# Selective scan: GpSimd forms a row's inputs for two channel blocks in one instruction, with its products four steps late and other buffer counts

## Chip, cores and metric

The kernel runs on one core of a Trainium2 chip. The metric is the device time of one execution in microseconds; of the kernel before there are three, of which the median stands in the table below.

## What is computed

The reference chains four layers over a stream of 1,024 rows of 256: grouped attention, a mixture of experts, a pair of Mamba passes (one forward, one over the reversed sequence), and a feed-forward layer whose weights are looked up in a table of 16 values. The change lies in the Mamba passes. Cut to that:

```python
def _selective_scan(xi, dt, Bm, Cm, A, D):        # per sequence: DI = 512 channels, DS = 16 states
    def step(h, inp):
        dt_t, B_t, C_t, x_t = inp
        dA = jnp.exp(dt_t[..., None] * A)
        h = dA * h + (dt_t * x_t)[..., None] * B_t[:, None, :]
        y = jnp.einsum('bds,bs->bd', h, C_t)
        return (h, y)
    ...
    return ys + xi * D
# around it: dt = softplus(dtr @ dt_w.T + dt_b);  y = scan(...) * silu(z);  y @ out_w.T
```

## The kernel before

**The scan's steps.** The 512 channels are four blocks of 128 partitions; the time axis of the four sequences is laid out in halves of 512 columns (two sequences of 256). Direction (2) times half (2) gives four segments, `seg`. A segment has 64 steps (`SSTEP`), and a step is one state of one channel block: an instruction of 128x512. Steps come in pairs of blocks: `place(n)` (L1026) says that 32 steps (`PSTEP`, called a pair) alternate between two blocks, b = 0 and b = 1, and go through the 16 states; two neighbouring steps share one row r = n // 2, since B and C are the same for both blocks. There are 256 steps and 128 rows. The steps of a segment's first 32 work on blocks 0 and 1, the others on blocks 2 and 3.

**One step through the engines.** ScalarE writes the decay exp(dt·A) into one of three PSUM banks, `da` (L1727 and L1728). GpSimd forms the input `uB` = u · B (L1649), where u = dt · x and the row of B was copied to all partitions by a DMA into `RB`. VectorE runs the recurrence along the row with one scan instruction, in place in `da` (L1799) or into `hS` in SBUF (L1796). The state is multiplied by the row of C (`RC`): on VectorE from `da` into `hV` (L1741) or, for the steps that `on_pool` (L1011) picks, on GpSimd from `hS` into `hP` (L1658). TensorE adds the product to the output bank `ya` with an identity matmul (L1818).

**What orders the work.** Each engine has one queue, written out by hand, and counts on semaphores. GpSimd issues the input of step n, then the product of step n - `LATE` where that is its own; it forms an input once the scan of step n - `UBUF` has ended. VectorE issues scan n, then `product(n-1)` if that is its own. ScalarE may write `da` n when step n - 3 has left the bank: after its scan, if GpSimd has the product, or else after VectorE's product. `hP` has `PBUF` buffers, `hV` has `CBUF`, `hS` has two. SyncE issues the row loads in one queue: B of row i, then C of row i - 2 (L1613 to L1623); a row buffer is refilled when both its steps are through.

```python
ROWS = 4
UBUF, CBUF, PBUF, DABUF = 3, 3, 2, 3
LATE = 2
def on_pool(n):
    return n % 8 in (1, 4, 6) and n % PSTEP < PSTEP - LATE      # 11 of 32 steps
```

**Work beside it.** Between the steps the engines carry out the next segment's preparation (`side_tensor`, `side_scalar`, `side_vector`), hung on step numbers: projections and convolution on TensorE, copies and activations on ScalarE (with table loads where SiLU takes turns with exp and log, L1324 and L1328), and on VectorE `softplus` (L1559: `dt` from its parts, then `u`, L1562 and L1564), `out_vector` and one `table_vector` (L1552, a subtraction of two SBUF tiles) at step 56 of the last segment. `gate` (L1743) multiplies a finished `ya` with silu(z) at steps 2 and 3 of the next 32. `xi`, `sz`, `dt` and `u` are held twice, by the parity of the segment.

Of the kernel before, what the change touches and what calls it, by code (L numbers as in the profile page):

```python
# [14 lines left out]
ALU = mybir.AluOpType  # L15
# [963 lines left out]
ROWS = 4  # L979
UBUF, CBUF, PBUF, DABUF = 3, 3, 2, 3  # L980
LATE = 2
# [29 lines left out]
def on_pool(n):  # L1011

    return n % 8 in (1, 4, 6) and n % PSTEP < PSTEP - LATE

# [7 lines left out]
def vector_steps(n):  # L1022
    return n - pool_steps(n)


def place(n):  # L1026

    pair = n // PSTEP
    return n // SSTEP, pair, 2 * (pair % 2) + n % 2, n % 2, n // 2, n // 2 % ROWS

# [36 lines left out]
def mamba(c, g, dram, wt, ws, acc, hh, hl, sc):  # L1067
# [16 lines left out]
    s_rb, s_rc = ([sem(f"row_{n}{i}") for i in range(ROWS)] for n in "bc")  # L1084
# [4 lines left out]
    with ExitStack() as ctx:  # L1089
# [270 lines left out]
        def keep_dt(e, k, d):  # L1360
            e.wait_ge(s_u, DB * k + d + 1)
            e.activation(dt[:, k % 2, d, :], DTB[d][:, :], ACT.Copy).then_inc(s_dtc, 1)
# [196 lines left out]
        def softplus(e, k, d):  # L1559
            e.wait_ge(s_ln, DB * k + d + 1)  # L1560
            e.wait_ge(s_mx, DB * k + d + 1)
            e.tensor_tensor(DTB[d][:, :], DTB[d][:, :], u[:, k % 2, d, :], ALU.add).then_inc(s_dt, 1)  # L1562
            e.wait_ge(s_dt, DB * k + d + 1)
            e.tensor_tensor(u[:, k % 2, d, :], DTB[d][:, :], xi[:, k % 2, d, :], ALU.mult).then_inc(s_u, 1)  # L1564
# [39 lines left out]
        with nc.Block() as block:  # L1604
            @block.sync
            def _(e):

                mamba_weights(c, dram, "bm", ws[1])
                rows = STEPS // 2
                row = lambda r, at: dram["bc"][at + r % DS:at + r % DS + 1, half_of(r // (SSTEP // 2))].broadcast_to([P, HALF])  # L1610
                for i in range(rows + BEHIND):
                    if i < rows:
                        if i % (SSTEP // 2) == 0:  # L1613
                            e.wait_ge(s_bc, 16 * (i // (SSTEP // 2) + 1))
                        if i >= ROWS:
                            e.wait_ge(s_ub, 2 * (i - ROWS) + 2)
                        e.dma_start(RB[:, i % ROWS, :], row(i, 0)).then_inc(s_rb[i % ROWS], 16)
                    r = i - BEHIND
                    if r >= 0:
                        if r >= ROWS:  # L1620
                            e.wait_ge(s_hv, vector_steps(2 * (r - ROWS) + 2))
                            e.wait_ge(s_hp, pool_steps(2 * (r - ROWS) + 2))
                        e.dma_start(RC[:, r % ROWS, :], row(r, DS)).then_inc(s_rc[r % ROWS], 16)  # L1623

            @block.gpsimd
            def _(e):
                e.memset(raw[:, :, :, 0:PADC], 0.0).then_inc(s_pad, 1)
                e.memset(raw[:, :, :, PADC + SEQ:], 0.0).then_inc(s_pad, 1)
                e.memset(sc.zero[:, :], 0.0).then_inc(s_pad, 1)

                e.wait_ge(s_cs, (DCONV - 1) * DB)
                e.wait_ge(s_dg, DB * PADC)
                for w in ws:
                    e.wait_ge(w.ready, w.count)
                    for d in range(DB):
                        e.tensor_scalar(w.dD[:, d, :], g.ident[:, :], w.Dv[:, d:d + 1], None,
                                        ALU.mult).then_inc(s_dd, 1)
                e.tensor_tensor(g.x[:, :, :], g.x[:, :, :], wt.b_out[:, :].unsqueeze(1).broadcast_to([P, NB, D]),
                                ALU.add).then_inc(s_res, 1)
                for n in range(STEPS + LATE):  # L1640
                    if n < STEPS:
                        seg, pair, d, b, r, q = place(n)
                        if n % PSTEP < 2:
                            e.wait_ge(s_u, DB * seg + d + 1)
                        if b == 0:
                            e.wait_ge(s_rb[q], 16 * (r // ROWS + 1))
                        if n >= UBUF:
                            e.wait_ge(s_sc, n - UBUF + 1)
                        e.tensor_tensor(uB[:, n % UBUF, :], u[:, seg % 2, d, :], RB[:, q, :],  # L1649
                                        ALU.mult).then_inc(s_ub, 1)  # L1650
                    m = n - LATE
                    if m >= 0 and on_pool(m):
                        k, (r, q) = pool_steps(m), place(m)[4:]
                        e.wait_ge(s_rc[q], 16 * (r // ROWS + 1))
                        e.wait_ge(s_sc, m + 1)
                        if k >= PBUF:
                            e.wait_ge(s_ap, k - PBUF + 1)
                        e.tensor_tensor(hP[:, k % PBUF, :], hS[:, k % 2, :], RC[:, q, :],  # L1658
                                        ALU.mult).then_inc(s_hp, 1)

            @block.scalar
            def _(e):
# [48 lines left out]
                for n in range(STEPS):  # L1711
                    seg, pair, d, b, r, q = place(n)
# [15 lines left out]
                    e.activation(to[:, :, rest], by_seq(dt[:, seg % 2, d, :])[:, :, rest], ACT.Exp,  # L1728
# [5 lines left out]
            def _(e):  # L1734
                def product(n):
                    k, (r, q) = vector_steps(n), place(n)[4:]
                    e.wait_ge(s_rc[q], 16 * (r // ROWS + 1))
# [3 lines left out]
                    e.tensor_tensor(hV[:, k % CBUF, :], da[n % DABUF][:, :], RC[:, q, :], ALU.mult).then_inc(s_hv, 1)  # L1741
# [38 lines left out]
                for n in range(STEPS):  # L1780
                    seg, pair, d, b, r, q = place(n)
# [7 lines left out]
                    e.wait_ge(s_ub, n + 1)  # L1789
                    way = slice(None) if seg < 2 else slice(None, None, -1)  # L1790
                    a = da[n % DABUF]
                    if on_pool(n):
                        k = pool_steps(n)
                        if k >= 2:
                            e.wait_ge(s_hp, k - 1)
                        e.tensor_tensor_scan(hS[:, k % 2, way], a[:, way], uB[:, n % UBUF, way], 0.0,  # L1796
                                             ALU.mult, ALU.add).then_inc(s_sc, 1)
                    else:
                        e.tensor_tensor_scan(a[:, way], a[:, way], uB[:, n % UBUF, way], 0.0,  # L1799
# [353 lines left out]
def build(nc, dram, out):  # L2153
    with ExitStack() as ctx:
# [62 lines left out]
        with ExitStack() as mm:  # L2217
# [19 lines left out]
            sc.xi, sc.sz, sc.dt, sc.u = (c.sb(mm, n, [P, 2, DB, HALF]) for n in ("xi", "sz", "dt", "u"))  # L2237
            sc.RB, sc.RC = c.sb(mm, "rows_B", [P, ROWS, HALF]), c.sb(mm, "rows_C", [P, ROWS, HALF])
            sc.uB, sc.hV, sc.hP = (c.sb(mm, n, [P, w, HALF]) for n, w in (("uB", UBUF), ("hV", CBUF), ("hP", PBUF)))
            sc.dtr = c.sb(mm, "dtr", [P, HALF])  # L2240
            sc.zero = c.sb(mm, "zero", [P, NHS])
            sc.hS, sc.e1 = c.over("hS", [P, 2, HALF], g.feat), c.over("e1", [P, 2, HALF], g.feat, skip=8 * HALF)
# [78 lines left out]
```

## Time and profile before

| what | value |
|---|---|
| runs of the kernel before | 1097.88, 1098.32, 1099.91 us; median 1098.32 us |
| profiled execution, its own time | 1099.44 us |
| its span in the profile | 1097.7 us |
| busy share of the span | PE 87%, DVE 80%, POOL 64%, ACT 51% |
| scan stage, first scan to last | 556.85 us to about 1017 us |
| mean granted TensorE clock | 0.953 |

The span is the time from the first to the last instruction in the profile; 1.7 us lie around it. PE is TensorE, DVE is VectorE, ACT is ScalarE, POOL is GpSimd, SPq is SyncE's DMA queue. The four layers run one after another, so the shares of the whole span average over stages; the scan stage, some 460 us, is read by itself. In the profile, a wait for several semaphores is put down to the one that the profile has coming last, and where that engine had long been done it was another.

### The profile page before, as it was taken

To read this page: it belongs to the slowest core of one execution; us is meant where nothing else is said; L and a number is where in the kernel's file an instruction comes from. 1 tells how busy PE (TensorE), PEld (TensorE's weight loads), DVE (VectorE), ACT (ScalarE), POOL (GpSimd) and SP (SyncE) were. 2 spreads that over 40 slices of the span, in tenths; PEclk is the share of its full clock that TensorE was granted. 3 is DMA by queue.
4 is the path that set the end of the run, shared out by engine and by line. 5 is a ranking of instruction groups with operands and counts; after the bars stand their busy time and mean duration, and the time that the engine had idled before them with its cause. 6 is when DMAs were issued, how large, how long until landed. Compare 5 with 4: busy or idle time off the path is not lost. (4 is left out here: it accounts for less than half of the span.)

```text
span 1097.7 us, 13218 instructions
## 1 busy us (share of the span) xinstructions
PE 959.0 (87%) x3836; PEld 600.4 (55%) x3836; DVE 873.2 (80%) x1136; ACT 560.8 (51%) x1204; POOL 703.3 (64%) x505
## 2 busy tenths in 40 slices
PE   5898867999999999995969977989889987787798
PEld 2566646888888888883424422433444342332487
DVE  3788677777778778776579899988998999999853
ACT  2687632333333333322667766766577467564141
POOL 3377623555555555541289799989998899999000
PEclk9899988999999999997979999989999899999999
DMA  3000025442442442313065555654545455664001
GB/s 102 1 2 0 1 110 152 123 134 82 119 134 88 112 134 94 108 39 91 13 161 155 163 152 145 147 161 142 153 140 157 125 146 154 153 154 115 0 1 39
DMA packets 60033, 115.32 MB, mean 105 GB/s; under 512 B 10400, under 2 KB 15776, under 8 KB 59856
## 3 DMA queue, kind: packets, MB, share of 16 engines
q1 hardware_dynamic: 58848, 112.87, 36.7%
q10 hardware_dynamic: 1136, 1.90, 0.5%
q8 instruction: 18, 0.29, 0.1%
q14 instruction: 31, 0.25, 0.1%
HBM read 113.24 MB, written 1.51 MB: 105 GB/s over the span
## 5 line engine op out<-in xcount | busy, mean ns | idle before, releaser
L1649 POOL TENSOR_TENSOR uB<-u,rows_B 128x512 f32<-128x512 f32 x256 | 320.4, 1282 | 17.1 <-DVE da L1799 13.7
L870 POOL TENSOR_TENSOR lutw<-lutw,lt 128x865 f32<-128x865 f32 x80 | 184.9, 2312 | 164.9 <-DVE lt L836 159.1
L1818 PE MATMUL ya<-hV,ident 128*128 128x512 f32 x336 | 189.6, 651 | 62.6 <-DVE hV L1741 61.9
L1799 DVE TENSOR_TENSOR_SCAN da<-da,uB 128x512 f32<-128x512 f32 x168 | 201.0, 1220 | 17.2 <-ACT da L1728 12.3
L1818 PEld LDWEIGHTS ya<-hV,ident 128*128 128x128 f32 x336 | 61.3, 201 | 158.9 <-DVE hV L1741 123.4
L1658 POOL TENSOR_TENSOR hP<-hS,rows_C 128x512 f32<-128x512 f32 x88 | 112.7, 1281 | 21.8 <-issue 8.5
L1727 ACT ACTIVATE da<-zero 128x2 f32<-128x2 f32 x256 | 43.0, 168 | 152.0 <-DVE hV L1741 151.7
L1796 DVE TENSOR_TENSOR_SCAN hS<-da,uB 128x512 f32<-128x512 f32 x88 | 106.7, 1212 | 16.0 <-ACT da L1727 7.5
L1741 DVE TENSOR_TENSOR hV<-da,rows_C 128x512 f32<-128x512 f32 x168 | 112.6, 671 | 0.0
L744 ACT ACTIVATE ah<-ups 128x1024 fp32r<-128x1024 f32 x40 | 41.2, 1029 | 130.0 <-DVE ups L832 130.0
L829 DVE TENSOR_TENSOR si<-gps,cwb 128x1024 f32<-128x1024 f32 x40 | 49.0, 1225 | 57.1 <-ACT gps L741 53.4
L1818 PE MATMUL ya<-hP,ident 128*128 128x512 f32 x176 | 93.6, 614 | 0.0
L1728 ACT ACTIVATE da<-dt,fm_A 128x510 f32<-128x510 f32 x128 | 86.2, 674 | 0.0
L1728 ACT ACTIVATE da<-dt,bm_A 128x510 f32<-128x510 f32 x128 | 86.1, 673 | 0.0
L741 ACT ACTIVATE gps<-gps 128x1024 f32<-128x1024 f32 x40 | 40.3, 1008 | 89.4 <-PE gps L880 89.4
L349 POOL TENSOR_TENSOR prob<-prob,ri 128x1024 f32<-128x1024 f32 x32 | 60.7, 1896 | 28.4 <-DVE ri L513 28.4
L880 PE MATMUL gps<-xh,wh 128*128 128x512 f32 x160 | 63.4, 396 | 5.6 <-DVE si L829 5.6
L584 ACT ACTIVATE prob<-sps,mx 128x256 f32<-128x256 f32 x128 | 59.0, 481 | 11.1 <-DVE mx L509 11.0
L832 DVE TENSOR_TENSOR ups<-ups,si 128x1024 f32<-128x1024 f32 x40 | 49.3, 1233 | 19.2 <-PE ups L880 19.2
L880 PE MATMUL gps<-xh,wl 128*128 128x512 f32 x160 | 63.0, 394 | 0.0
L880 PE MATMUL gps<-xl,wh 128*128 128x512 f32 x160 | 63.0, 394 | 0.0
L880 PE MATMUL ups<-xh,wh 128*128 128x512 f32 x160 | 62.3, 390 | 0.0
(341 smaller groups left out, 2034.8 us busy)
## 6 DMA issues: line engine op xcount, KB each, us to landing
rows_B<-bc_rows SPq DMA_DIRECT2D x128, 256.0 KB, 3.6
rows_C<-bc_rows SPq DMA_DIRECT2D x128, 256.0 KB, 4.3
wr<-in_moe_w SPq DMA_DIRECT2D x40, 384.0 KB, 4.8
cwb<-cw_rows SPq DMA_DIRECT2D x16, 512.0 KB, 4.0
cwb<-cw_rows SPq DMA_DIRECT2D x16, 384.0 KB, 5.0
cwb<-cw_rows SPq DMA_DIRECT2D x16, 256.0 KB, 4.1
lut_f<-in_lut_idx SPq DMA_DIRECT2D x1, 2160.0 KB, 10.3
cwb<-cw_rows SPq DMA_DIRECT2D x16, 128.0 KB, 4.4
```

Of the source, the lines that this page charges most:

```text
L349: e.tensor_tensor(prob[:, u % NP, :, :], prob[:, u % NP, :, :], ri[:, u, :].unsqueeze(2).broadcast_to([P, GROUPS, SEQ]), ALU.mult).then_in ...
L584: a = e.activation(prob[:, u % NP, gg, :], sps[:, u % 2, gg, :], ACT.Exp, bias=mx[:, u, gg:gg + 1], accum_out=rs[:, u, gg:gg + 1])
L832: e.tensor_tensor(ups[:, :], ups[:, :], si[:, s, :], ALU.mult).then_inc(s_a, 1)
L870: e.tensor_tensor(part, part, lt[:, q, :], ALU.add).then_inc(s_la, 1)
L880: mm = e.matmul(ps[:, half(h)], w[:, slot, o:o + P], x[:, q, half(h)], start=i == 0, stop=i == len(terms) - 1)
L1649: e.tensor_tensor(uB[:, n % UBUF, :], u[:, seg % 2, d, :], RB[:, q, :], ALU.mult).then_inc(s_ub, 1)
L1658: e.tensor_tensor(hP[:, k % PBUF, :], hS[:, k % 2, :], RC[:, q, :], ALU.mult).then_inc(s_hp, 1)
L1728: e.activation(to[:, :, rest], by_seq(dt[:, seg % 2, d, :])[:, :, rest], ACT.Exp, scale=ws[seg // 2].A[:, d, r % DS:r % DS + 1]).then_inc( ...
L1741: e.tensor_tensor(hV[:, k % CBUF, :], da[n % DABUF][:, :], RC[:, q, :], ALU.mult).then_inc(s_hv, 1)
L1796: e.tensor_tensor_scan(hS[:, k % 2, way], a[:, way], uB[:, n % UBUF, way], 0.0, ALU.mult, ALU.add).then_inc(s_sc, 1)
L1799: e.tensor_tensor_scan(a[:, way], a[:, way], uB[:, n % UBUF, way], 0.0, ALU.mult, ALU.add).then_inc(s_sc, 1)
L1818: return e.matmul(ya[n % 2][:, :], g.ident[:, :], at, start=False, stop=False, skip_group_check=True).then_inc(done, 1)
```

## The change

GpSimd's loop runs over rows, not steps: one instruction of 128 x (2 x 512) multiplies u of both blocks with the row of B, broadcast over the blocks. The products that GpSimd has are issued four steps behind, not two. `on_pool` picks other steps, 12 of 32 in place of 11. `dt` and `u` are held once. Buffers: B rows 4 to 3, C rows 4 to 5, inputs 3 steps to 3 rows (6 steps), `hV` 3 to 4, `hP` 2 to 3, `hS` 2 to 4; `da` stays at 3. `hS` gets its own memory, and `dtr` moves over `g.feat`.

```diff
-ROWS = 4
-UBUF, CBUF, PBUF, DABUF = 3, 3, 2, 3
-LATE = 2
+BROWS, CROWS = 3, 5
+UPAIRS, CBUF, PBUF, DABUF, HBUF = 3, 4, 3, 3, 4
+LATE = 4
...
-    return n % 8 in (1, 4, 6) and n % PSTEP < PSTEP - LATE
+    return n % PSTEP % 7 in (1, 3, 5) and n % PSTEP < PSTEP - LATE
...
-            e.activation(u[:, k % 2, d, :], DTB[d][:, :], ACT.Relu, ...)
+            e.activation(u[:, d, :], DTB[d][:, :], ACT.Relu, ...)
...
-                        if i >= ROWS:
-                            e.wait_ge(s_ub, 2 * (i - ROWS) + 2)
-                        e.dma_start(RB[:, i % ROWS, :], row(i, 0)).then_inc(s_rb[i % ROWS], 16)
+                        if i >= BROWS:
+                            e.wait_ge(s_ub, i - BROWS + 1)
+                        e.dma_start(RB[:, i % BROWS, :], row(i, 0)).then_inc(s_rb[i % BROWS], 16)
                     r = i - BEHIND
                     if r >= 0:
-                        if r >= ROWS:
-                            e.wait_ge(s_hv, vector_steps(2 * (r - ROWS) + 2))
-                            e.wait_ge(s_hp, pool_steps(2 * (r - ROWS) + 2))
+                        if r >= CROWS:
+                            e.wait_ge(s_hv, vector_steps(2 * (r - CROWS) + 2))
+                            e.wait_ge(s_hp, pool_steps(2 * (r - CROWS) + 2))
...
-                for n in range(STEPS + LATE):
-                    if n < STEPS:
-                        seg, pair, d, b, r, q = place(n)
-                        if n % PSTEP < 2:
-                            e.wait_ge(s_u, DB * seg + d + 1)
-                        if b == 0:
-                            e.wait_ge(s_rb[q], 16 * (r // ROWS + 1))
-                        if n >= UBUF:
-                            e.wait_ge(s_sc, n - UBUF + 1)
-                        e.tensor_tensor(uB[:, n % UBUF, :], u[:, seg % 2, d, :], RB[:, q, :],
-                                        ALU.mult).then_inc(s_ub, 1)
-                    m = n - LATE
-                    if m >= 0 and on_pool(m):
...
+                for r in range((STEPS + LATE) // 2):
+                    if 2 * r < STEPS:
+                        seg, pair, d = place(2 * r)[:3]
+                        if r % DS == 0:
+                            e.wait_ge(s_u, DB * seg + d + 2)
+                        e.wait_ge(s_rb[r % BROWS], 16 * (r // BROWS + 1))
+                        if r >= UPAIRS:
+                            e.wait_ge(s_sc, 2 * (r - UPAIRS) + 2)
+                        e.tensor_tensor(uB[:, r % UPAIRS, :, :], u[:, d:d + 2, :],
+                                        RB[:, r % BROWS, :].unsqueeze(1).broadcast_to([P, 2, HALF]),
+                                        ALU.mult).then_inc(s_ub, 1)
+                    for m in (2 * r - LATE, 2 * r - LATE + 1):
+                        if m >= 0 and on_pool(m):
+                            k, row = pool_steps(m), place(m)[4]
+                            e.wait_ge(s_rc[row % CROWS], 16 * (row // CROWS + 1))
+                            e.wait_ge(s_sc, m + 1)
+                            if k >= PBUF:
+                                e.wait_ge(s_ap, k - PBUF + 1)
+                            e.tensor_tensor(hP[:, k % PBUF, :], hS[:, k % HBUF, :], RC[:, row % CROWS, :],
+                                            ALU.mult).then_inc(s_hp, 1)
...
                     e.wait_ge(s_da, 2 * n + 2)
-                    e.wait_ge(s_ub, n + 1)
+                    e.wait_ge(s_ub, r + 1)
...
-                        if k >= 2:
-                            e.wait_ge(s_hp, k - 1)
-                        e.tensor_tensor_scan(hS[:, k % 2, way], a[:, way], uB[:, n % UBUF, way], 0.0,
+                        if k >= HBUF:
+                            e.wait_ge(s_hp, k - HBUF + 1)
+                        e.tensor_tensor_scan(hS[:, k % HBUF, way], a[:, way], uB[:, r % UPAIRS, b, way], 0.0,
...
-            sc.xi, sc.sz, sc.dt, sc.u = (c.sb(mm, n, [P, 2, DB, HALF]) for n in ("xi", "sz", "dt", "u"))
+            sc.xi, sc.sz = (c.sb(mm, n, [P, 2, DB, HALF]) for n in ("xi", "sz"))
+            sc.dt, sc.u = (c.sb(mm, n, [P, DB, HALF]) for n in ("dt", "u"))
```

## Rows read from the trace of the kernel before

**Rows 1.** Busy time of each engine in stretches; the second sums 18 stretches, 556.8 to 1018.
```profile
800.00:848.60 48.60, 46.88 (x117) 21.18 (x115) 43.60 (x48) 37.21 (x82) 45.69 (x37) 1.00 0.51 149
...
sum 461.20, PE 393.06 PEld 164.31 DVE 427.86 ACT 298.78 POOL 423.11; mean PE 21.84 PEld 9.13 DVE 23.77 ACT 16.60 POOL 23.51
```
**Rows 2.** Costliest groups of instructions, the scan's on POOL and DVE.
```profile
L1649 POOL TENSOR_TENSOR uB<-u,rows_B 128x512 f32<-128x512 f32 x256 | 320.4, 1282 | 17.1 <-DVE da L1799 13.7
...
L1799 DVE TENSOR_TENSOR_SCAN da<-da,uB 128x512 f32<-128x512 f32 x168 | 201.0, 1220 | 17.2 <-ACT da L1728 12.3
...
L1658 POOL TENSOR_TENSOR hP<-hS,rows_C 128x512 f32<-128x512 f32 x88 | 112.7, 1281 | 21.8 <-issue 8.5
...
L1741 DVE TENSOR_TENSOR hV<-da,rows_C 128x512 f32<-128x512 f32 x168 | 112.6, 671 | 0.0
```
**Rows 3.** Waits of DVE from 554 to 1018 us: total, times, longest.
```profile
DVE da L1799 <- ACT da L1728: 12.3, 8, 2.8
DVE hS L1796 <- ACT da L1727: 7.5, 19, 0.6
DVE hS L1796 <- issue: 6.5, 3, 2.5
DVE da L1799 <- POOL uB L1649: 2.8, 6, 1.3
DVE hS L1796 <- ACT da L1728: 1.8, 3, 0.8
DVE da L1799 <- ACT da L1727: 1.8, 6, 0.3
```
**Rows 4.** Timeline of DVE, 742 to 756: start, duration, instructions, [idle before].
```profile
743.62 0.67 DVE L1741 TENSOR_TENSOR hV<-da,rows_C 128x512 f32<-128x512 f32 x1
744.20 2.34 DVE L1799 TENSOR_TENSOR_SCAN da<-da,uB 128x512 f32<-128x512 f32 x2
746.44 0.68 DVE L1741 TENSOR_TENSOR hV<-da,rows_C 128x512 f32<-128x512 f32 x1
749.65 1.22 DVE L1796 TENSOR_TENSOR_SCAN hS<-da,uB 128x512 f32<-128x512 f32 x1 [2.53 <-issue]
...
754.56 1.22 DVE L1796 TENSOR_TENSOR_SCAN hS<-da,uB 128x512 f32<-128x512 f32 x1 [0.27 <-ACT da L1727]
```
**Rows 5.** Timeline of POOL, the same stretch.
```profile
747.07 1.27 POOL L1658 TENSOR_TENSOR hP<-hS,rows_C 128x512 f32<-128x512 f32 x1 [2.34 <-PE ya L1818]
748.30 3.72 POOL L1649 TENSOR_TENSOR uB<-u,rows_B 128x512 f32<-128x512 f32 x3
751.98 1.27 POOL L1658 TENSOR_TENSOR hP<-hS,rows_C 128x512 f32<-128x512 f32 x1
753.21 3.72 POOL L1649 TENSOR_TENSOR uB<-u,rows_B 128x512 f32<-128x512 f32 x3
```
**Rows 6.** Groups of POOL instructions by shape: other products and sums.
```profile
L870 POOL TENSOR_TENSOR lutw<-lutw,lt 128x865 f32<-128x865 f32 x80 | 184.9, 2312 | 164.9 <-DVE lt L836 159.1
...
L349 POOL TENSOR_TENSOR prob<-prob,ri 128x1024 f32<-128x1024 f32 x32 | 60.7, 1896 | 28.4 <-DVE ri L513 28.4
...
L1638 POOL TENSOR_TENSOR x<-x,b_out 128x2048 f32<-128x2048 f32 x1 | 4.5, 4521 | 0.0
```
**Rows 7.** Timeline of the scan's start.
```profile
554.26 5.16 POOL L1649 TENSOR_TENSOR uB<-u,rows_B 128x512 f32<-128x512 f32 x4 [3.17 <-DVE u L1564]
554.82 0.69 DVE L1564 TENSOR_TENSOR u<-side,xi 128x512 f32<-128x512 f32 x1
...
556.85 1.23 DVE L1799 TENSOR_TENSOR_SCAN da<-da,uB 128x512 f32<-128x512 f32 x1 [1.33 <-POOL uB L1649]
```
**Rows 8.** Timeline around step 56 of the last segment, DVE.
```profile
1003.25 3.64 DVE L1552 TENSOR_TENSOR lut_l<-lutw,lut_h 128x540 fp32r<-128x540 f32 x1
```
**Rows 9.** The same stretch, POOL.
```profile
1002.57 3.73 POOL L1649 TENSOR_TENSOR uB<-u,rows_B 128x512 f32<-128x512 f32 x3
```
**Rows 10.** DMA issues of the page: KB each, us from issue to landing.
```profile
rows_B<-bc_rows SPq DMA_DIRECT2D x128, 256.0 KB, 3.6
```

More of the change, by code:

```diff
@@ L1028, in place @@
     pair = n // PSTEP
-    return n // SSTEP, pair, 2 * (pair % 2) + n % 2, n % 2, n // 2, n // 2 % ROWS
+    return n // SSTEP, pair, 2 * (pair % 2) + n % 2, n % 2, n // 2
 def summed(pair):
@@ L1082, in mamba @@
         sem, "xb bcc bc xl lr dm ab e1 ln mx dt dtc u".split())
-    s_rb, s_rc = ([sem(f"row_{n}{i}") for i in range(ROWS)] for n in "bc")
+    s_rb, s_rc = ([sem(f"row_{n}{i}") for i in range(w)] for n, w in (("b", BROWS), ("c", CROWS)))
     s_da, s_ub, s_sc, s_hv, s_hp, s_av, s_ap, s_sk, s_g, s_om, s_oa = map(
@@ L1348, in parts @@
             e.activation(e1[:, d % 2, :], DTB[d][:, :], ACT.Abs, bias=ws[k // 2].dtb[:, d:d + 1]).then_inc(s_ab, 1)
-            e.activation(u[:, k % 2, d, :], DTB[d][:, :], ACT.Relu, bias=ws[k // 2].dtb[:, d:d + 1]).then_inc(s_mx, 1)
+            e.activation(u[:, d, :], DTB[d][:, :], ACT.Relu, bias=ws[k // 2].dtb[:, d:d + 1]).then_inc(s_mx, 1)
         def exp(e, k, d):
@@ L1361, in keep_dt @@
             e.wait_ge(s_u, DB * k + d + 1)
-            e.activation(dt[:, k % 2, d, :], DTB[d][:, :], ACT.Copy).then_inc(s_dtc, 1)
+            e.activation(dt[:, d, :], DTB[d][:, :], ACT.Copy).then_inc(s_dtc, 1)
         def silu_input(e, k):
@@ L1561, in softplus @@
             e.wait_ge(s_mx, DB * k + d + 1)
-            e.tensor_tensor(DTB[d][:, :], DTB[d][:, :], u[:, k % 2, d, :], ALU.add).then_inc(s_dt, 1)
+            e.tensor_tensor(DTB[d][:, :], DTB[d][:, :], u[:, d, :], ALU.add).then_inc(s_dt, 1)
             e.wait_ge(s_dt, DB * k + d + 1)
-            e.tensor_tensor(u[:, k % 2, d, :], DTB[d][:, :], xi[:, k % 2, d, :], ALU.mult).then_inc(s_u, 1)
+            e.tensor_tensor(u[:, d, :], DTB[d][:, :], xi[:, k % 2, d, :], ALU.mult).then_inc(s_u, 1)
         def side_vector(e, seg):
@@ L1711, in _ @@
                 for n in range(STEPS):
-                    seg, pair, d, b, r, q = place(n)
+                    seg, pair, d, b, r = place(n)
                     if n % SSTEP == 0:
@@ L1727, in _ @@
                     e.activation(to[:, :, first], sc.zero[:, :], ACT.Copy).then_inc(s_da, 1)
-                    e.activation(to[:, :, rest], by_seq(dt[:, seg % 2, d, :])[:, :, rest], ACT.Exp,
+                    e.activation(to[:, :, rest], by_seq(dt[:, d, :])[:, :, rest], ACT.Exp,
                                  scale=ws[seg // 2].A[:, d, r % DS:r % DS + 1]).then_inc(s_da, 1)
@@ L1735, in product @@
                 def product(n):
-                    k, (r, q) = vector_steps(n), place(n)[4:]
-                    e.wait_ge(s_rc[q], 16 * (r // ROWS + 1))
+                    k, r = vector_steps(n), place(n)[4]
+                    e.wait_ge(s_rc[r % CROWS], 16 * (r // CROWS + 1))
                     if k >= CBUF:
@@ L1740, in product @@
                     e.wait_ge(s_sc, n + 1)
-                    e.tensor_tensor(hV[:, k % CBUF, :], da[n % DABUF][:, :], RC[:, q, :], ALU.mult).then_inc(s_hv, 1)
+                    e.tensor_tensor(hV[:, k % CBUF, :], da[n % DABUF][:, :], RC[:, r % CROWS, :],
+                                    ALU.mult).then_inc(s_hv, 1)
                 def gate(pair, b):
@@ L1780, in _ @@
                 for n in range(STEPS):
-                    seg, pair, d, b, r, q = place(n)
+                    seg, pair, d, b, r = place(n)
                     if n % SSTEP == 0:
@@ L2236, in build @@
             sc.win_in, sc.xp_in = c.kept("win_in"), c.kept("xp_in")
-            sc.xi, sc.sz, sc.dt, sc.u = (c.sb(mm, n, [P, 2, DB, HALF]) for n in ("xi", "sz", "dt", "u"))
-            sc.RB, sc.RC = c.sb(mm, "rows_B", [P, ROWS, HALF]), c.sb(mm, "rows_C", [P, ROWS, HALF])
-            sc.uB, sc.hV, sc.hP = (c.sb(mm, n, [P, w, HALF]) for n, w in (("uB", UBUF), ("hV", CBUF), ("hP", PBUF)))
-            sc.dtr = c.sb(mm, "dtr", [P, HALF])
+            sc.xi, sc.sz = (c.sb(mm, n, [P, 2, DB, HALF]) for n in ("xi", "sz"))
+            sc.dt, sc.u = (c.sb(mm, n, [P, DB, HALF]) for n in ("dt", "u"))
+            sc.RB, sc.RC = c.sb(mm, "rows_B", [P, BROWS, HALF]), c.sb(mm, "rows_C", [P, CROWS, HALF])
+            sc.uB = c.sb(mm, "uB", [P, UPAIRS, 2, HALF])
+            sc.hV, sc.hP, sc.hS = (c.sb(mm, n, [P, w, HALF]) for n, w in (("hV", CBUF), ("hP", PBUF), ("hS", HBUF)))
             sc.zero = c.sb(mm, "zero", [P, NHS])
-            sc.hS, sc.e1 = c.over("hS", [P, 2, HALF], g.feat), c.over("e1", [P, 2, HALF], g.feat, skip=8 * HALF)
+            sc.dtr, sc.e1 = c.over("dtr", [P, HALF], g.feat), c.over("e1", [P, 2, HALF], g.feat, skip=8 * HALF)
             sc.bcr = c.over("bcr", [2 * DS, HALF], g.feat, skip=12 * HALF)
```

11 lines of the change are left out of this document (2 added, 9 removed).

## The prediction

> **What bounds the kernel now.** The change touches the scan stage alone, so I read that stage. The busy time by stretches comes first: of the 461 us from 556.8 to 1018, DVE is busy for 428 and POOL for 423 [rows 1]. Two engines in series, each at 92%, and some 33 us of idle time on DVE: the question is who ends it. The groups of instructions give the work [rows 2]: POOL does 256 inputs and 88 products at 1.28 us, DVE 256 scans at about 1.22 and 168 products at 0.67. An instruction starts a little before its predecessor's end, so I take pitches from the timelines. Two scans take 2.24 us from 744.20 to 746.44 and a product 0.58 from 743.62 to 744.20 [rows 4], so a scan costs DVE 1.12 us and a product 0.585. Three inputs take 3.68 from 748.30 to 751.98, and a product 1.23 from 751.98 to 753.21 [rows 5], so everything on POOL costs 1.23.
>
> Per step DVE then wants 1.12 + 168/256 x 0.585 = 1.50 us before its work beside the scan; POOL wants 344 x 1.23 / 256 = 1.65. POOL is the slower one wherever DVE has nothing else to do, and DVE wherever it has softplus, gates or a late decay. With inputs only three steps deep, neither can run ahead to cover the other.
>
> The waits of DVE say how much each costs, once their labels are corrected [rows 3]. The scan at 754.56 is put down to ACT's small copy (L1727), but the input that POOL began at 753.21 ends 1.28 later, at 754.49 [rows 4, 5]: that is what it waited for. The two scans that waited, 749.65 and 754.56, are 4.91 us apart, as are the beginnings of POOL's groups of inputs, 748.30 and 753.21: four POOL instructions, to the hundredth. So the 7.5 + 1.8 us under L1727 are waits for POOL. The 6.5 us in three waits named "issue" are too: before the one at 749.65, POOL's product had waited 2.34 us for TensorE to free one of two `hP` buffers, and the next input stood behind it in POOL's queue, from 748.30 to 749.5 [rows 4, 5]. Of the 2.8 us under uB, 1.33 are the start of the scan [rows 7] and 1.5 are POOL. In all **17.3 us of DVE's idle time are POOL's**. The 12.3 + 1.8 us under L1728 are real waits for ACT, mostly behind its SiLU and table loads (the longest is 2.8).
>
> **The change part by part.** *Inputs in pairs.* 256 instructions at 1.23 become 128 of 1,024 elements. No row has this instruction; its bounds are L349 with 1,024 elements but a second operand held constant along 256 columns, 1.90 us, and two of today's, 2 x 1.28 = 2.56 [rows 6, 2]. The nearest is L1638, which like the new one has a row broadcast over blocks: 2,048 elements in 4.52 us. The line through 512 at 1.282 and 2,048 at 4.521 has 2.109 ns per element and 0.20 us fixed, so 2.36 us, pitch 2.31. POOL falls by 128 x (2.46 - 2.31) = 19 us.
>
> *Twelve products of 32 in place of eleven.* 96 for 88: POOL gains 8 x 1.23 = 10 us of work, DVE loses 8 x 0.585 = **4.7 us**, all on the path where DVE sets the pace. POOL's total is 128 x 2.31 + 96 x 1.23 = 414 us (423 before); DVE's is 428 - 4.7 = 423. Per step POOL wants 1.62 and DVE 1.12 + 160/256 x 0.585 = 1.49.
>
> *Inputs three rows deep, products four steps late.* POOL may form the input of row r+1 when row r-2 is scanned, while DVE still has rows r-1 and r ready: about 2 x 3.1 = 6.2 us of DVE's work. In that time POOL needs at most one product and one input, 3.5 us. So it has 2.7 us to spare, against a lag of 0.13 us a step: 20 steps, and in 20 steps DVE has a softplus pair or a gate nearly everywhere in the schedule of work beside. With three `hP` buffers in place of two, POOL's product at 747.07 would not have waited for the last add but one. I remove all 17.3 us.
>
> *The start.* A first input now needs u of both blocks. The second u ends at 554.82 + 0.69 = 555.51, and the pair takes 2.36: 557.9, where the first scan began at 556.85 [rows 7]. That costs **1.1 us**. Later, both u are written at DVE's steps 23 to 25 and 52, 53, and POOL may take them from steps 28 and 60 on, so this wait is covered by two steps at least; if softplus came three steps later it would show.
>
> *Waits for ACT.* Three decay banks remain, so 14.1 us stay. But DVE will meet ACT's other side jobs where it met POOL before. Where a step on POOL stands between two on DVE, ACT has one scan, 1.12 us, from the bank's release to the next scan, and 11 such places in 32 become 12. The range is from nothing to the 8 us that half a microsecond at one place in six would make; I take **3 us**, nearer to nothing, since waits under L1728 outside the big ones are few today [rows 3].
>
> *Single dt and u.* ACT overwrites u and dt of block d some 15 steps after their last reader; costs nothing, and if it did wait, ACT would stand still with the decays behind it. *Row buffers.* B of row i is issued when the input of row i-3 ends, and wanted two inputs and at least one product later, 2 x 2.31 + 1.23 = 5.9 us; it lands in 3.6 [rows 10] and is ready. SyncE issues as many DMAs in the same order; the C row's wait, for row r-5's products, has always been met by then. `hS` and `dtr` change places only.
>
> *The table subtraction.* At 1003.25 DVE's subtraction of two SBUF tiles took 3.64 us [rows 8], while POOL ran three inputs from 1002.57 to 1006.30 [rows 9]: it ended 0.6 us after them. It waited until POOL stopped, through more than one instruction. With POOL's pieces longer, what POOL can still do before it needs a scan is from one product (1.2) to two pairs and two products (7.1); the wait was 2.9, so between -1.7 and +4.2, and I take **+1**. The Trainium skill (SBUF — State Buffer, SBUF: two separate sides) says that the shared port pair goes to whichever "starts first" for the whole instruction, with the other blocked. By that rule alone the wait would have ended with the first input at about 1003.85 and would now be at most one pair, 2.36 us, which makes the sum a microsecond or two lower; the trace agrees that one blocks, not that it lasts only one instruction.
>
> **The sum.** -17.3 - 4.7 + 1.1 + 3 + 1 = -16.9 us. The profiled span of 1097.7 becomes 1080.8 and that execution's 1099.44 becomes 1082.5. It stands 1.1 us above the median of 1098.32, so against the median I predict **1081.4 us**, 1.5% less. A measurement of this kernel can tell about 0.2% from no change.
>
> **The rivals.** *B, POOL remains the pacemaker.* If the pair costs two singles, POOL's total is 128 x 2.51 + 96 x 1.23 = 439 us; with perhaps a third of its 38 idle us left (12, around the start and ACT's long jobs) the stage is 451 against 461: 1088.5. For it speaks that today's price per element is 2.5 ns; against it, L1638's 2.2 and L349's 1.85.
>
> *C, another engine takes over.* From 800 to 848.6 TensorE is busy for 46.9 of 48.6 us at full clock [rows 1]; there are three such stretches, and its side work feeds ACT and so the decays. If it or ACT catches every wait that POOL leaves, only the 8 products and the start count: -3.6, 1094.7. Against it: TensorE idles in the other half of each segment, where most of the 17.3 us lie, and ACT is busy for 299 of 461 [rows 1].
>
> *D, slower.* The price of the pair decides. The 865-element sum of L870 takes 2.31 us [rows 6], 2.67 ns per element; at that, a pair is 2.74, POOL's total 128 x 2.69 + 118 = 462, with 12 idle 474: +13, or 1111 us. The point is a pair at 2.63 us. Against it: L870 stands beside other DVE work and in L1638 more elements take less each. The Trainium skill (Perfetto Trace Analysis, Optimizing Scalar/DVE Operations) warns that moving work between DVE and GpSimd "might not help", since they share a read port. Here DVE's scans and products read one operand from PSUM, and a product on DVE takes 0.67 us on the average of 168 [rows 2]; no run here shows them slowed.
>
> **The numbers.** The forecast 0.68, B 0.12, C 0.12, D 0.08. The forecast's own range is from 1074 (nothing for ACT, the table at its low end, POOL cheaper) to 1090 (8 for ACT, the table at its high end). The 8-in-10 range takes in B and stops short of C's centre and D: 1072 to 1094. All of the forecast and B, and most of C, are faster by over 0.2% (2.2 us): 0.88. Within 0.2%: 0.05, from C with a little more lost. Slower: 0.07.
>
> **What would show it.** Right: L1649's group x128 near 2.36 us; waits of scans named L1727, uB and "issue" down from 17.3 to a few us; waits named L1728 between 14 and 20; products on DVE x160; no long wait of POOL for TensorE ahead of an input. Wrong: a pair at 2.5 us or more, with POOL busy for over 95% of the stage; scans waiting for rows of B; DVE's products waiting for TensorE's adds, or the decays for TensorE's convolution between steps 10 and 30.

## The result, and the profile after

The changed kernel takes 1103.35 us (median of six runs, 1101.18 to 1104.36) against 1098.2 before: a ratio of 1.0043, 95% interval 1.0030 to 1.0055. I had forecast 1081.4 and a range of 1072 to 1094. It is slower, outside the range and on the other side.

The costliest groups of the page after (the same columns as in [rows 2]):

```profile
L1649 POOL TENSOR_TENSOR uB<-u,rows_B 128x1024 f32<-128x1024 f32 x128 | 301.1, 2361 | 15.3 <-DVE da L1801 10.7
...
L1801 DVE TENSOR_TENSOR_SCAN da<-da,uB 128x512 f32<-128x512 f32 x160 | 192.5, 1219 | 26.7 <-ACT da L1729 23.8
...
L1659 POOL TENSOR_TENSOR hP<-hS,rows_C 128x512 f32<-128x512 f32 x96 | 122.2, 1273 | 33.1 <-DVE hS L1798 24.8
...
L1742 DVE TENSOR_TENSOR hV<-da,rows_C 128x512 f32<-128x512 f32 x160 | 106.9, 669 | 0.0
```

The waits of DVE in the scan stage, from 554 to 1024 us, to be held against [rows 3]:

```profile
DVE da L1801 <- ACT da L1729: 23.8, 16, 2.7
DVE hS L1798 <- ACT da L1729: 14.4, 16, 1.7
...
DVE da L1801 <- POOL uB L1649: 2.5, 1, 2.5
```

And the waits of ACT in the same stretch, of which there were 5.9 us for PE before:

```profile
ACT e L1348 <- PE side L1205: 7.1, 3, 2.4
ACT sz L1313 <- PE side L1109: 6.6, 4, 2.2
ACT xi L1298 <- PE side L1132: 6.3, 10, 1.2
ACT bcr L1334 <- PE side L1177: 5.3, 3, 1.8
ACT dtr L1342 <- PE side L1188: 4.6, 3, 1.5
ACT raw L1292 <- PE side L1109: 4.3, 7, 1.3
```

GpSimd did all that was expected of it. The paired input takes 2.361 us (2.36 forecast), and the only wait for it that is left is the first of the scan. In its place VectorE waits 38.2 us for ScalarE's exponentials, the decays (L1729; it was L1728, 14.1 us). ScalarE has no more work than before (busy for 297.8 us of the stage, 298.8 before); it stands 34.2 us before TensorE's side results, and the next decay stands behind it in its queue.

The timeline of PE at the beginning of the second segment after the change shows where that begins:

```profile
679.14 1.12 PE L1820 MATMUL ya<-hV,ident 128*128 128x512 f32 x2 [1.38 <-DVE hV L1742]
683.79 2.08 PE L1820 MATMUL ya<-hV,ident 128*128 128x512 f32 x2 [3.52 <-DVE hV L1742]
685.66 1.91 PE L1205 MATMUL side<-dtr,wdt 128*128 128x512 f32 x2
687.37 1.39 PE L1875 MATMUL ya<-xi,fm_dD 128*128 128x512 f32 x2
```

ScalarE and VectorE at that place, also after the change:

```profile
687.61 0.69 ACT L1348 ACTIVATE e<-side,fm_dtb 128x512 f32<-128x512 f32 x1 [2.35 <-PE side L1205]
```

```profile
689.58 1.23 DVE L1801 TENSOR_TENSOR_SCAN da<-da,uB 128x512 f32<-128x512 f32 x1 [1.30 <-ACT da L1729]
```

And PE at the same place before:

```profile
680.42 1.12 PE L1818 MATMUL ya<-hV,ident 128*128 128x512 f32 x2 [1.39 <-DVE hV L1741]
681.39 1.02 PE L1873 MATMUL ya<-xi,fm_dD 128*128 128x512 f32 x2
682.24 1.02 PE L1818 MATMUL ya<-hV,ident 128*128 128x512 f32 x2
683.10 1.02 PE L1205 MATMUL side<-dtr,wdt 128*128 128x512 f32 x2
```

TensorE's side work hangs on the number of adds done (`side.advance(pair % 2 * PSTEP + i)`), not on the step. `summed` puts a GpSimd product's add `LATE` steps behind. With `LATE` = 2 the third add is that of step 3; with `LATE` = 4 and the new places it is that of step 4, the fourth that of step 5 (was 3), the fifth that of step 6 (was 5). Counted out over 32 adds, they come 0.8 step later on the average, and the side work with them. Here the third dt matmul (L1205) comes only behind the add of step 4, after a gap of 3.5 us. ScalarE waits 2.35 us for it (the row at 687.61), VectorE 1.30 for the next decay (689.58). The same wait of ScalarE stands at the beginning of the third and the fourth segment.

### The profile page after: what moved, and what is told of

It is laid out like the page before. It is cut to its first block and busy times, and to the rows that moved or that the text cites. A ratio compares the mean times of both kernels' runs of the same rounds, so it can differ in the third digit from the quotient of the medians.

```text
span 1102.6 us, 13081 instructions
## 1 busy us (share of the span) xinstructions
PE 959.8 (87%) x3836; PEld 602.7 (55%) x3836; DVE 869.6 (79%) x1128; ACT 561.1 (51%) x1204; POOL 694.1 (63%) x385
## 5 line engine op out<-in xcount | busy, mean ns | idle before, releaser
L1649 POOL TENSOR_TENSOR uB<-u,rows_B 128x1024 f32<-128x1024 f32 x128 | 301.1, 2361 | 15.3 <-DVE da L1801 10.7
L1820 PE MATMUL ya<-hV,ident 128*128 128x512 f32 x320 | 181.4, 652 | 72.0 <-DVE hV L1742 72.0
L1801 DVE TENSOR_TENSOR_SCAN da<-da,uB 128x512 f32<-128x512 f32 x160 | 192.5, 1219 | 26.7 <-ACT da L1729 23.8
L1820 PEld LDWEIGHTS ya<-hV,ident 128*128 128x128 f32 x320 | 57.9, 199 | 162.3 <-DVE hV L1742 127.6
L1659 POOL TENSOR_TENSOR hP<-hS,rows_C 128x512 f32<-128x512 f32 x96 | 122.2, 1273 | 33.1 <-DVE hS L1798 24.8
L1798 DVE TENSOR_TENSOR_SCAN hS<-da,uB 128x512 f32<-128x512 f32 x96 | 116.1, 1209 | 14.6 <-ACT da L1729 14.4
L1728 ACT ACTIVATE da<-zero 128x2 f32<-128x2 f32 x256 | 42.8, 167 | 128.1 <-DVE hV L1742 126.0
L1742 DVE TENSOR_TENSOR hV<-da,rows_C 128x512 f32<-128x512 f32 x160 | 106.9, 669 | 0.0
L1820 PE MATMUL ya<-hP,ident 128*128 128x512 f32 x192 | 103.0, 619 | 0.0
L1729 ACT ACTIVATE da<-dt,fm_A 128x510 f32<-128x510 f32 x128 | 86.3, 674 | 0.0
L1729 ACT ACTIVATE da<-dt,bm_A 128x510 f32<-128x510 f32 x128 | 86.2, 673 | 0.0
L584 ACT ACTIVATE prob<-sps,mx 128x256 f32<-128x256 f32 x128 | 59.0, 481 | 11.1 <-DVE mx L509 11.0
L832 DVE TENSOR_TENSOR ups<-ups,si 128x1024 f32<-128x1024 f32 x40 | 49.3, 1233 | 19.3 <-PE ups L880 19.2
```

Source lines behind the costliest of these rows:

```text
L584: a = e.activation(prob[:, u % NP, gg, :], sps[:, u % 2, gg, :], ACT.Exp, bias=mx[:, u, gg:gg + 1], accum_out=rs[:, u, gg:gg + 1])
L832: e.tensor_tensor(ups[:, :], ups[:, :], si[:, s, :], ALU.mult).then_inc(s_a, 1)
L1649: e.tensor_tensor(uB[:, r % UPAIRS, :, :], u[:, d:d + 2, :], RB[:, r % BROWS, :].unsqueeze(1).broadcast_to([P, 2, HALF]), ALU.mult).then_i ...
L1659: e.tensor_tensor(hP[:, k % PBUF, :], hS[:, k % HBUF, :], RC[:, row % CROWS, :], ALU.mult).then_inc(s_hp, 1)
L1729: e.activation(to[:, :, rest], by_seq(dt[:, d, :])[:, :, rest], ACT.Exp, scale=ws[seg // 2].A[:, d, r % DS:r % DS + 1]).then_inc(s_da, 1)
L1798: e.tensor_tensor_scan(hS[:, k % HBUF, way], a[:, way], uB[:, r % UPAIRS, b, way], 0.0, ALU.mult, ALU.add).then_inc(s_sc, 1)
```

## The experiments

Theory T1: the lag of that count makes the change slow. Rivals: T2, TensorE is simply full; T3, the new places of GpSimd's steps free the decay banks late. Times are medians; the kernel before stood at 1097.8 to 1098.6 beside them, and ratios are to it. "The decay's waits" are VectorE's waits for ScalarE's exponentials.

**1. Side work one add earlier.**

```diff
-                        side.advance(pair % 2 * PSTEP + i)
+                        side.advance(pair % 2 * PSTEP + min(i + 1, PSTEP - 1))
```

> The changed kernel, with TensorE's side work hung one add earlier in each 32 steps. Theory T1 (TensorE's side jobs are counted in adds; with products four steps late the count lags the steps by up to two, so ScalarE stands before TensorE's results and the decays come late): ScalarE's waits for TensorE's side results fall from 34 us to under 15, VectorE's waits for the decay exponential from 38 us to 18 to 25, time 1083 to 1092. T2 (TensorE is simply full in the stretches with projection and convolution): nothing comes earlier, the same waits within 5 us, time 1099 to 1105. T3 (it is the places of GpSimd's steps, each alone between two of VectorE's, which free the decay banks late): waits stay, time 1100 to 1105.

1088.9 us, ratio 0.9920 [0.9904, 0.9937]: 14.5 less than the change. ScalarE's waits for TensorE are 8.2 us, VectorE's for the decay 20.6. As T1 has it, waits and time; T2 and T3, each as the whole cause, have no room for this.

**2. Products two steps late.**

```diff
-LATE = 4
+LATE = 2
-    return n % PSTEP % 7 in (1, 3, 5) and n % PSTEP < PSTEP - LATE
+    return n % PSTEP % 7 in (1, 3, 5) and n % PSTEP < PSTEP - 4
```

> The changed kernel with GpSimd's products two steps late, not four (the same 12 steps of 32, all other buffer counts kept). T1: TensorE's count of adds follows the steps again; VectorE's waits for the decay exponential fall to 18 to 25 us, time 1083 to 1092, perhaps with some 5 us more of waits for GpSimd, which runs one row less ahead. T2 and T3: VectorE's waits for the decay stay at 33 us or more, time 1098 to 1106.

1099.1 us, 1.0013 [0.9999, 1.0026]. The time lies in the range of T2 and T3, the waits are T1's. ScalarE's waits for TensorE fell to 6.2 us and the decay's (L1729) to 17.9, as T1 says, but GpSimd now stood 41.8 us before its products for scans just under way, and the inputs behind them came late. The waits of its DVE from 554 us on, where the small ones labelled L1728 are again GpSimd's:

```profile
DVE da L1801 <- POOL uB L1649: 11.7, 19, 2.5
DVE da L1801 <- ACT da L1729: 9.8, 5, 2.7
DVE hS L1798 <- ACT da L1729: 8.1, 8, 1.7
DVE hS L1798 <- ACT da L1728: 6.6, 12, 0.6
```

So with the new places the four steps are needed for GpSimd's lead, and harm TensorE's count.

**3. The pairs without the rest** (old places, products two steps late, old counts of `hV`, `hP`, `hS`).

```diff
-UPAIRS, CBUF, PBUF, DABUF, HBUF = 3, 4, 3, 3, 4
-LATE = 4
+UPAIRS, CBUF, PBUF, DABUF, HBUF = 3, 3, 2, 3, 2
+LATE = 2
-    return n % PSTEP % 7 in (1, 3, 5) and n % PSTEP < PSTEP - LATE
+    return n % 8 in (1, 4, 6) and n % PSTEP < PSTEP - LATE
```

> The paired inputs and their three rows of buffers, single dt and u and the row buffers of the change, but the old 11 steps of 32, products two steps late, and the old counts of hV, hP and hS. T1: waits for the decay near the 14 us of before, GpSimd's waits mostly gone but for the ones behind two hP buffers (6.5 us); 8 products more on VectorE than in the change: 1083 to 1090. T2: 1098 to 1104. T3: as T1, since the old places are back: 1083 to 1090, so this run tells T2 from the other two, and the run with products two steps late tells T1 from T3.

1092.75 us, 0.9946 [0.9930, 0.9963]; ScalarE waits 4.6 us for TensorE. The pairs alone gain 5.5 us, outside the 1083 to 1090 that I had written: the decay's waits are 17.4 us, not near 14, and 8.4 us of GpSimd's are left behind the first scan. It speaks against T2, which wanted 1098 to 1104.

**4. The new places alone**, in the kernel before.

```diff
-    return n % 8 in (1, 4, 6) and n % PSTEP < PSTEP - LATE
+    return n % PSTEP % 7 in (1, 3, 5) and n % PSTEP < PSTEP - 4
```

> The kernel before with the 12 steps of 32 of the change and nothing else. GpSimd sets the pace there and gets 8 products of 1.23 us more, so up to 10 us slower. T1 and T2: 1102 to 1109, with VectorE's waits for the decay exponential (the true ones) within 4 us of the 14 of before. T3: the true waits for the decay grow by 10 us or more, time 1109 or above.

1113.0 us, 1.0130 [1.0113, 1.0147], slower than any branch of the text but T3's, whose mark, 10 us more of waits for the decay, is missing: they are 17.6 us (14.1 before), and ScalarE waits 1.9 for TensorE. Waits that are GpSimd's rose by 12 us, as the pacemaker got 10 us more work. A part of T3 is real, and has its row, here in this run and in the kernel before: the wait behind the gate's SiLU, three times in each.

```profile
685.66 1.22 DVE L1796 TENSOR_TENSOR_SCAN hS<-da,uB 128x512 f32<-128x512 f32 x1 [1.70 <-ACT da L1728]
```

```profile
683.20 1.23 DVE L1799 TENSOR_TENSOR_SCAN da<-da,uB 128x512 f32<-128x512 f32 x1 [1.12 <-ACT da L1728]
```

Step 3 of the 32 is now GpSimd's, and VectorE has a product less to cover ScalarE. Here GpSimd sets the pace and hides what the places cost otherwise; runs 5 to 8 show more of it.

**5. Old places in the change** (27 added, so 11 of 32, none in the last four), **6. with side work one add earlier, 7. two adds earlier; 8. new places, two adds earlier.**

```diff
-    return n % PSTEP % 7 in (1, 3, 5) and n % PSTEP < PSTEP - LATE
+    return (n % 8 in (1, 4, 6) or n % PSTEP == 27) and n % PSTEP < PSTEP - LATE
-                        side.advance(pair % 2 * PSTEP + i)
+                        side.advance(pair % 2 * PSTEP + min(i + 1, PSTEP - 1))
```

The first part is the edit of run 5; two adds earlier has `i + 2` in the second.

> The changed kernel with GpSimd's steps at the old places (n % 8 in 1, 4, 6, to which step 27 is added, so 11 of 32, none in the last four); products four steps late as in the change. T1: the count of adds still lags, so ScalarE still waits over 20 us for TensorE and the time is 1096 to 1105, 8 products more on VectorE included (5 us). T3 (the new places are the cause): waits for the decay back to 14 to 18 us, 1084 to 1090.

> Old places as in the run before this, and TensorE's side work hung one add earlier. T1 with a smaller part for the places (the alternation of the new ones lengthens the wait behind the gate's SiLU from 1.13 to 1.70 us, and others of its kind): 1086 to 1092, the 5 us of 8 more products nearly made up by 3 to 4 us less of waits for the decay. T3 as a large part: under 1084.

> The changed kernel with the old places and TensorE's side work two adds earlier. One add earlier gave 1084.1 us with 2 us of ScalarE's waits for TensorE left, so no lag remains: the decays' waits stay at 11 us, and adds that come later behind side work lengthen the gates' waits (7.5 us now). 1083 to 1089, no better than 1084.1.

> The changed kernel, with TensorE's side work hung two adds earlier. Hung one add earlier it gave 1088.9 us and left 11 us of ScalarE's waits for TensorE. T1 (the count): those fall further, VectorE's waits for the decay exponential from 20.6 to 15 to 18 us, 1084 to 1088. T2 (TensorE full in the dense stretches): no further gain, and side work ahead of the adds makes gates and GpSimd's product buffers wait longer: 1088 to 1095.

In this order: 1091.9, 1084.1, 1086.75 and 1086.0 us; ratios 0.9948 [0.9932, 0.9964], **0.9870 [0.9848, 0.9893]**, 0.9889 [0.9873, 0.9905], 0.9874 [0.9843, 0.9904]. With the change and run 1 they make a table; each field has the time, the decay's waits and ScalarE's waits for TensorE, in us. The times are medians, the waits those of the profiled execution, which was the slowest for runs 7 and 8 (1089.4 and 1090.0 us).

| side work | new places | old places |
|---|---|---|
| as in the change | 1103.35; 38.2; 34.2 | 1091.9; 19.0; 18.7 |
| one add earlier | 1088.9; 20.6; 8.2 | 1084.1; 11.1; 1.7 |
| two adds earlier | 1086.0; 23.1; 3.4 | 1086.75; 6.2; 3.5 |

Run 5 lies between T1's 1096 and T3's 1090: the places act on the count too, which I had not worked out. With the old ones the third add is that of step 3 again, and the 2.35 us before L1205 are gone; 18.7 us of ScalarE's waits are left, and the shift takes them to 1.7. The average lag there is 0.7 step, counted as above, hardly less than the new places' 0.8: what matters is which adds are late, not the average.

Run 6 is faster than T1's branch (1086 to 1092) and stands at the edge of "T3 as a large part" (under 1084). Run 8 has T1's time, but not its waits: the decay's were to fall to 15 to 18 and are 23.1, although ScalarE hardly waits for TensorE any more. So with the lag mostly out of the way the new places still cost waits for the decay: 9.5 us one add earlier (20.6 against 11.1), twice what their eight products fewer on VectorE save, hence 1088.9 us against 1084.1; and 16.9 us two adds earlier, where ScalarE waits as little for TensorE with either (there VectorE stands longer before GpSimd and the gates with the old ones, and the times are equal). The wait behind the gate's SiLU, step 5 of the 32, is 1.70 us three times in runs 1 and 8, whatever the shift, and 0.6 us twice in run 6. With the old places two adds earlier buys nothing beyond one (run 7, as expected in its time). Run 6 is the fastest kernel of this study and beats both. Its DVE's waits:

```profile
DVE da L1801 <- ACT da L1729: 11.1, 10, 2.7
DVE sz L1751 <- issue: 6.5, 5, 2.8
DVE da L1801 <- POOL uB L1649: 2.5, 1, 2.5
```

**9. TensorE with less to do.** Two of the convolution's three matmuls are left out in segments 1 to 3.

```diff
                 if t:
                     yield
+                if t < PADC - 1:
+                    continue
```

> The changed kernel with two of the convolution's three diagonal matmuls left out on TensorE in segments 1 to 3 (that part of the computation is left out, all waits and yields stay), some 7 us less of TensorE's work in each dense stretch. T2 (TensorE full): ScalarE's waits for TensorE go in those stretches, time 1090 or less. T1: only the waits for the convolution's own results shrink (6.3 us), while those at the beginning of a segment, where TensorE has idle time, stay: 1096 to 1101.

1098.2 us, 1.0004 [0.9992, 1.0015]. Of ScalarE's 34.2 us before TensorE 26.8 stay. Those for the convolution (L1132, 6.3 us) are gone, and those for L1205 at a segment's beginning stay: 2.35, 2.35 and 2.21 us, against 2.35, 2.35 and 2.36. As T1 has it; T2 falls, which wanted 1090 or less.

**10. and 11. The kernel before, with side work one add later and one earlier.**

```diff
-                        side.advance(pair % 2 * PSTEP + i)
+                        side.advance(pair % 2 * PSTEP + (max(i - 1, 0) if i < PSTEP - 1 else i))
```

> The kernel before with nothing changed but that TensorE's side work hangs one add later. Counted, the change ran its adds 0.8 step later than the kernel before on the average of 32; this run puts that lag into the kernel before. T1: ScalarE's waits for TensorE rise from 6 us to 20 or more and the time by 6 to 14 us, to 1104 to 1112. If something else in the change was the cause: within 3 us of 1098.

> The kernel before with TensorE's side work hung one add earlier. There GpSimd sets the pace and ScalarE waits only 6 us for TensorE: 1096 to 1099, no gain beyond 2 us. If side work one add earlier were a gain of its own, whatever the change: under 1092, and the good times of the runs with the shift would not speak for the lag.

1094.95 us (0.9975 [0.9963, 0.9987]) and 1107.6 us (1.0083 [1.0063, 1.0103]): both against what I had written. The link is there: one add later, ScalarE waits 20.6 us for TensorE in place of 5.9 and the decay's waits go from 14.1 to 21.7. But the three waits named "issue", 6.5 us, that came of GpSimd standing before two `hP` buffers [rows 3, 5] fell to 0.4, as the adds come ahead of the side work. One add earlier it is the reverse: ScalarE never waits for TensorE, and "issue" is 11.3 us. GpSimd's own waits for TensorE's adds go the same way, 5.5 us before, 3.0 one add later and 14.4 one add earlier. Early side work pays only where GpSimd has buffers to spare.

**12. Inputs two rows deep** in the fastest version (`UPAIRS` = 2).

> Old places, TensorE's side work one add earlier (1084.1 us), and inputs two rows deep instead of three. If the depth of the inputs is what removed VectorE's waits for GpSimd: they come back to 10 us or more, 1092 to 1100. If the cheaper instruction did (2.36 us for two inputs in place of 2.56): 1084 to 1087.

1098.3 us, 1.0000 [0.9987, 1.0012], 14.2 more than with three. It is the depth that pays, not the cheaper instruction: GpSimd has the same 2.36 us an input, and waits 53 us for scans to free one (16.5 with three rows). Some 9 us of VectorE's waits for it are back, a little under the 10 of the first branch.

**13. Gates a step later** in the fastest version (`GATE_AT` = 3).

> Old places, side work one add earlier, and the gates one step later (steps 3 and 4 of the next 32), since VectorE still stood 7.5 us before gates for TensorE's last adds. If it only waits for the adds: half of that goes, 1080 to 1083. If the next 32 steps' adds, which wait for the gate to free the bank, then fill hV's four buffers: 1084 to 1090.

1086.4 us, 0.9886 [0.9863, 0.9908], in the second branch. The gates' waits fall from 7.5 to 4.6 us, the decay's rise from 11.1 to 15.1. Nothing gained.

**14. ScalarE's side jobs a step later**, TensorE as in the change.

```diff
-                    side.advance(n % SSTEP)
+                    side.advance(n % SSTEP - 1)
```

> The changed kernel with ScalarE's side jobs one step later and TensorE's program untouched. If ScalarE stands before TensorE's late results and holds up the decays (T1): its waits for TensorE's side results fall from 34 us to 10 to 20, VectorE's waits for the decay exponential from 38 to 22 to 30, time 1089 to 1097. If earlier side work on TensorE helped in another way (adds, gates, product buffers): ScalarE's jobs later only push its results out, 1101 to 1107.

1102.3 us, 1.0040 [1.0027, 1.0052]. The waits moved as T1 said, the time, in the other branch's range, did not: ScalarE's for TensorE 34.2 to 17.5, VectorE's for the decay 38.2 to 17.2. But VectorE's own side jobs, whose due steps were left, now stand before ScalarE's results:

```profile
DVE acc L1557 <- PE side L1218: 6.8, 5, 2.0
DVE wl_in L1546 <- ACT wh_in L1284: 5.1, 4, 2.1
...
DVE side L1562 <- ACT side L1358: 3.8, 9, 0.8
```

The side work is one timetable over three engines.

**15. The count restored**: after each add, as much side work as the old order of adds had released by that step.

```diff
+                was = times(lambda n: n % 8 in (1, 4, 6) and n < PSTEP - 2, 2)
+                due = [sum(t <= now for t in was) - 1 for now in times(on_pool, LATE)]
...
-                        side.advance(pair % 2 * PSTEP + i)
+                        side.advance(pair % 2 * PSTEP + due[i])
```

(`times(on, late)` lists the step at which each add is issued.)

> The changed kernel with TensorE's side work at the step numbers that it had in the kernel before: after each add, as much of it as the old order of adds had released by that step. T1, with the lag of the count as the whole of it: ScalarE's waits for TensorE under 12 us, VectorE's waits for the decay exponential 16 to 22 us, 1084 to 1091. If one add earlier gained by more than undoing the lag: 1092 or above, clearly worse than 1088.9.

1095.8 us, 0.9975 [0.9966, 0.9985]: 7.6 of the 14.5 us, and outside T1's branch. ScalarE's waits for TensorE are 19.5 us (under 12 expected), the decay's 27.2 (16 to 22). The count could not be restored everywhere: step 3 no longer has an add, so what was due there still waits for step 4's, and the 2.35 us before L1205 stand in it unchanged. By the other branch one add earlier gains by more than undoing the lag; no run separates the two.

**16. One job earlier**: L1205 due at add 1 in segments 1 to 3 (`yield 2` to `yield 1` in `side_tensor`), all else as in the change.

> The changed kernel with one side job of TensorE in each of segments 1 to 3, the matmul for dt of block 2, due at add 1 in place of add 2, so before the gap behind the gate's SiLU. If that gap with the lowered clock is what makes the results late at the beginning of a segment: ScalarE's wait of 2.35 us for it (7.1 in all) goes, with it VectorE's waits of 1.30 us at that place (three) and perhaps part of the next ones (1.45): 1096 to 1100. If the waits at that place come from elsewhere: 1101 to 1105.

1096.4 us, 0.9984 [0.9974, 0.9994]: 7 us less than the change, for one job moved in three segments. ScalarE's waits for L1205 are gone and its others stay (27.0 us in all); the decay's are 33.7 us, 4.5 less. The rows at the gap:

```profile
678.27 1.02 PE L1205 MATMUL side<-dtr,wdt 128*128 128x512 f32 x2
682.04 1.24 PE L1820 MATMUL ya<-hV,ident 128*128 128x512 f32 x2 [2.75 <-DVE hV L1742]
```

## Why the prediction was wrong

*The pair.* Right: 2.361 us against 2.36, from the line through 512 and 2,048 elements.

*The 17.3 us.* Right, and so was reading L1727 and "issue" as GpSimd's: none of them is left in the change. It takes the depth: with two rows some 9 us of such waits are back (run 12).

*Products.* x160 of 669 ns, so 4.7 us of work less, right; but the same places cost more in waits (below). *The start.* The second u ends at 556.31 and the scan begins at 558.83, 1.98 us later than before; 0.8 of that lies ahead of the stage, where nothing was changed, 1.2 is the pair (1.1 forecast).

*The table subtraction.* 5.82 us in place of 3.64: +2.2 (+1 taken, within the bounds).

*Waits for ACT.* **This is the step that failed: 3 us taken, 8 at most allowed, 24.1 measured.** I had worked out when a decay bank comes free and looked for ScalarE's own work ahead of it; the 3 us were for that. I costed "products four steps late" on GpSimd's queue alone, though the same constant sets the order of TensorE's adds, and the adds are the clock of its side work. What the diff moved on TensorE's queue, some 110 side matmuls a segment by 0.8 step, was in no term. My rival C had the right sign of trouble and a wrong reason, that TensorE be full (run 9), and its price, at most what GpSimd gave back, was a bound that doesn't exist: a late job holds up ScalarE, ScalarE the decay, and VectorE stands although GpSimd is ready. The prediction's own sign of it, decays that wait for the convolution between steps 10 and 30, came in a small part: 6.3 of ScalarE's 34.2 us are for L1132.

The terms as measured: -17.3 - 4.7 + 1.2 + 24.1 + 2.2 + 0.8 ahead of the stage = +6.3 us; the span rose by 4.9. The 1.4 between them I leave open.

Of the waits for the decay the lag of the count is the greater part: one add earlier takes 17.6 of the 38.2 us away, and 14.5 us of time. The other part is in the term as I had it, and mis-sized: a step on GpSimd gives ScalarE less cover, which is read from the rows behind the SiLU (runs 1, 4, 6 and 8) and was not tested by itself. With side work one add earlier the new places have 9.5 us more of these waits than the old ones (runs 1 and 6), where I had taken 3 and allowed 8, and the eight products moved to GpSimd win nothing back. The two parts start from 11.1 us, the waits of run 6, not from the 14.1 before; and the split is that of this order, since the places move the count as well (run 5: taken first, they are 19.2 us and the count 7.9). Runs 10 and 11 set the limit of the theory: the lag costs its full price only where GpSimd no longer paces the scan.

## What to carry to other kernels

When one engine's schedule is counted in its own instructions, a change of their order is a change of its clock: list at which step each add falls, old and new, and which job hangs on it, before pricing the change. A wait that goes on the pacing engine is gained only if every queue that feeds the next bound keeps its dates; look there first for who stands in order ahead of the critical instruction. And buffers, lateness and due steps are one setting: here the change with nothing else but the old places and side work one add earlier goes from 0.4% slower to 1.3% faster.

## What the runs showed of the hardware

VectorE's subtraction of two SBUF tiles (L1552) waited through three further GpSimd instructions, beyond the one under way when it began. DVE, then POOL, of the changed kernel around 1006 us:

```profile
1006.29 5.82 DVE L1552 TENSOR_TENSOR lut_l<-lutw,lut_h 128x540 fp32r<-128x540 f32 x1
```

```profile
1006.75 1.26 POOL L1659 TENSOR_TENSOR hP<-hS,rows_C 128x512 f32<-128x512 f32 x1
1007.98 2.33 POOL L1649 TENSOR_TENSOR uB<-u,rows_B 128x1024 f32<-128x1024 f32 x1
1010.28 1.25 POOL L1659 TENSOR_TENSOR hP<-hS,rows_C 128x512 f32<-128x512 f32 x1
```

It ends 0.6 us after GpSimd's last and takes 0.71 where it does not wait. A wait of one pair at most, which the prediction weighed beside its own, is not what the trace shows.

TensorE's granted clock behind the gap of the second segment, in the changed kernel (columns: stretch, length, busy PE, PEld, DVE, ACT, POOL, then the granted clock, DMA share and GB/s) and at that place before:

```profile
683.70:688.50 4.80, 4.71 (x6) 2.04 (x7) 4.58 (x6) 2.37 (x6) 4.80 (x3) 0.54 0.49 119
```

```profile
682.00:688.00 6.00, 5.52 (x16) 2.84 (x16) 4.88 (x6) 4.41 (x11) 5.55 (x5) 1.00 0.61 128
```

After a wait of 3.52 us the clock stood near its lower level, 1.2 GHz, and L1205's two matmuls took 1.91 us for 1.02. So a job hung behind the gap was late twice. From the add's start to the end of L1205 it took 3.78 us here (683.79 to 687.57) and 1.88 before (682.24 to 684.12); at the earlier pace ScalarE, free at 685.26, would have waited some 0.4 us, so by this estimate 1.9 of the 2.35 us are the lowered clock. Moving the job ahead (run 16) took it out of both the gap and the lowered clock behind it, and cannot tell them apart. For the whole stage the place is the larger cause all the same: of the 34.2 us only 11.3 stand at a lowered clock, the three waits for L1205 (a granted clock of 0.50 while ScalarE stands) and two of 2.1 us for L1109 at step 59 (0.73 and 0.71); in the others it is 1.00.
